# Loads moved between queues, a third place for transposed x, and one more block's products ahead of the table gather

## The reference, cut to what matters

```
# layer 0: base product plus the batch's own adapter, added to x
result = jnp.einsum('bsd,od->bso', x, base_weight) + base_bias
h = jnp.einsum('bsd,brd->bsr', x, lora_A_w[adapter_ids0])
result = result + jnp.einsum('bsr,bor->bso', h, lora_B_w[adapter_ids0])
x = x + result
# layer 1: adapter alone, added to x
Bx = jnp.einsum('bni,bri->bnr', x, L1_cond_B[adapter_ids1])
x = x + jnp.einsum('bnr,bor->bno', Bx, L1_cond_A[adapter_ids1])
```

## Time and profile before

| | us |
|---|---|
| median of 3 runs | 98.51 |
| lowest, highest | 98.11, 99.58 |
| the profiled execution's own time | 97.92 |
| its span, first to last instruction | 95.8 |

### The profile page before, as it was taken

The page is one execution under the profiler, slowest core; times in us unless marked ns, Lnnn a source line. Parts: engine busy times, 40 slices in busy tenths (PEclk is TensorE's granted clock), DMA queues, the critical chain, the costliest instruction groups (busy, mean ns, idle before and its releaser), DMA issues.

```text
span 95.8 us, 2305 instructions
## 1 busy us (share of the span) xinstructions
PE 91.5 (96%) x662; PEld 90.0 (94%) x662; DVE 64.8 (68%) x120; ACT 58.7 (61%) x189; POOL 58.0 (61%) x126
## 2 busy tenths in 40 slices
PE   5999999999999999999999999999999999999980
PEld 5899999999899998999999999999999999999970
DVE  4499799227076468959587877768595868786460
ACT  0074598874588796748494948567584949480210
POOL 6504008850568999999576584959585766808500
PEclk9999999999999999999999999999999999999998
DMA  2999998968896289989996499992836354520205
GB/s 40 312 347 387 374 403 262 281 156 214 215 224 223 53 250 238 310 249 235 203 290 218 70 319 209 238 269 91 228 44 229 34 213 54 200 110 0 110 0 219
DMA packets 16335, 19.45 MB, mean 203 GB/s; under 512 B 1444, under 2 KB 11556, under 8 KB 16164
## 3 DMA queue, kind: packets, MB, share of 16 engines
q1 hardware_dynamic: 15040, 14.04, 50.1%
q0 software_dynamic: 1280, 5.28, 22.1%
q10 hardware_dynamic: 4, 0.00, 0.0%
HBM read 13.47 MB, written 5.84 MB: 202 GB/s over the span
## 4 chain that ended last, share of the span: by engine, by line
PE 90%; DVE 4%; ACT 2%; issue 1%; DVEq 0%; ACTq 0%
PE psum L394 55%; PE psum L440 11%; PE psum L432 4%; PE psum L362 4%; PE psum L480 4%; PE psum L378 4%; PE psum L370 3%; DVE table_rounded L640 3%; PE psum L466 2%; PE psum L414 1%; PE psum L405 1%; PE psum L448 1%; DVE y L679 1%; ACT row_ends L558 1%; ACT table_rounded L558 1%
## 5 line engine op out<-in xcount | busy, mean ns | idle before, releaser
L394 PE MATMUL psum<-wd,xt 128*128 128x256 f32 (+1 forms) x384 | 62.3, 310 | 0.0
L394 PEld LDWEIGHTS psum<-wd,xt 128*128 128x128 f32 x384 | 56.1, 188 | 0.0
L558 ACT ACTIVATE wd<-table_rounded 128x128 fp32r x128 | 27.7, 297 | 14.7 <-PE psum L394 12.5
L339 POOL TENSOR_TENSOR up_rows<-gathered_rows,up_rows 128x512 fp32r<-128x512 f32 x16 | 20.6, 1289 | 14.0 <-ACT up_rows L558 14.0
L322 POOL DMA_INDIRECT gathered_rows<-by_rank,rows x16 | 15.9, 996 | 6.3 <-DMA by_rank<-row_ends 3.8
L640 DVE TENSOR_TENSOR xt<-psum,xt 128x512 fp32r<-128x512 f32 x16 | 11.1, 691 | 6.6 <-ACT xt L558 5.9
L647 DVE STREAM_TRANSPOSE psum<-x_squares 128x512 f32<-128x512 f32 x13 | 14.4, 1110 | 0.0
L440 PE MATMUL psum<-up_rows,u_sel 128*128 128x256 f32 x96 | 14.2, 284 | 0.0
L440 PEld LDWEIGHTS psum<-up_rows,u_sel 128*128 128x128 f32 x96 | 12.8, 190 | 0.2
L659 DVE STREAM_TRANSPOSE psum<-psum 128x128 f32<-128x128 f32 x16 | 5.3, 330 | 11.2 <-PE psum L394 7.8
L332 POOL TENSOR_TENSOR g_sel<-gathered_rows,batch_mask 128x16 f32<-128x16 f32 x64 | 12.1, 227 | 0.9 <-DMA gathered_rows<-by_rank,rows 0.7
(11 more groups left out here) (60 smaller groups left out, 72.1 us busy)
## 6 DMA issues: line engine op xcount, KB each, us to landing
out<-y SPq DMA_DIRECT2D x15, 256.0 KB
x_squares<-in_x SPq DMA_DIRECT2D x8, 256.0 KB
w_rows<-in_L_cond_base_weight SPq DMA_DIRECT2D x4, 256.0 KB, 4.0
bw_rows<-in_L_cond_lora_B_w SPq DMA_DIRECT2D x1, 1024.0 KB, 7.0
a_rows<-in_L_cond_lora_A_w SPq DMA_DIRECT2D x1, 1024.0 KB, 9.2
by_rank<-bw_by_rank SPq DMA_DIRECT2D x4, 256.0 KB
x_squares<-in_x SPq DMA_DIRECT2D x8, 128.0 KB
x_rows<-in_x SPq DMA_DIRECT2D x3, 256.0 KB, 9.3
```

Source lines behind the costliest of these rows:

```text
L339: nc.gpsimd.tensor_tensor(out=up_rows[:, k % 2, LO, :], in0=gathered_rows[:, k % GATHERS, 0:D], in1=up_rows[:, k % 2, HI, :], op=ALU.subtr ...
L394: last = nc.tensor.matmul(bank_of(k, half)[:, start:end], xt[:, k % 2, c, x_part, :], wd[:, w_part, c, col:col + end - start], start=(c == ...
L558: return nc.scalar.activation(dst, src, ACT.Copy)
```

## The change

- SP no longer issues the loads of the broadcast adapter numbers (`ids_all`, two DMAs) and of the bias (`bias_all`). ACT issues them: the numbers before its first drain, the bias after `w_high(0)`. ACT's own reading of the first adapter numbers (`first`) comes after the bias.
- ACT makes a one-column copy (`table_call`) first of all, and drains `b1` in DVE's place.
- On SP, `load_x(1)`, `load_x(2)` and layer 1's A (`l1_a`) are issued ahead of layer 0's A.
- `xt` has three places. x's transpose for block 2 moves ahead of `g`, and block 2's plain half ahead of block 0's adapter half. That half is now made in one piece, with the adapter columns in all four chunks.
- Five `WARM_UPS` in place of six; the two `FILLERS` are gone.
- DVE drains `bw3` after `xt_low(1)`. ACT's `xt_high(2)` comes ahead of the first selections; `select(2, L1)` comes after `up_high(0)`, and `xt_high(3)` after `u_high(0)`. DVE's `xt_low(2)` comes before the reduction, `x_turn(3)` after `own_u(0)`.
- Blocks 4 and 5 of x are loaded apart, and the later groups are issued at other blocks.
- `up(0)` sits after three of block 2's four chunks, where it sat after two.

The core of the diff:

```diff
-WARM_UPS = 6
-FILLERS = 2
+X_SLOTS = 3
+WARM_UPS = 5
-X_GROUPS = ((0, 1), (1, 2), (2, 3), (3, 4), (4, 6), (6, 8), (8, 12), (12, 16))
+X_GROUPS = ((0, 1), (1, 2), (2, 3), (3, 4), (4, 5), (5, 6), (6, 8), (8, 12), (12, 16))
...
-        xt = sb("xt", [P, 2, C, 2, P], F32R)
+        xt = sb("xt", [P, X_SLOTS, C, 2, P], F32R)
...
             sp.dma_start(bw_rows[:, :, :], lora_b.rearrange("n (c p) r -> (n c) p r", p=P)).then_inc(bw_in, 16)
-            sp.dma_start(a_rows[:, :, :], lora_a.rearrange("(g n) r d -> (n r) g d", g=C)).then_inc(a_in, 16)
             load_x(1)
+            load_x(2)
             sp.wait_ge(a1_zeroed, 1)
...
-            load_x(2)
-            for layer, ids_of in ((L0, ids0), (L1, ids1)):
...
+            sp.dma_start(a_rows[:, :, :], lora_a.rearrange("(g n) r d -> (n r) g d", g=C)).then_inc(a_in, 16)
...
             load_x(3)
+            load_x(4)
             for k in range(NBLK - 1):
-                if k in (0, 1, 3, 6):
-                    load_x(4 + (0, 1, 3, 6).index(k))
+                if k in (1, 2, 3, 6):
+                    load_x(5 + (1, 2, 3, 6).index(k))
...
             w_fill(0)
-            keep_warm(FILLERS)
             wait_drained(pe, "b1")
...
             base(0, range(C), halves=[0])
+            x_fill(2)
...
             base(1, range(C), halves=[1])
-            x_fill(2)
+            wait_x(2)
+            wait_drained(pe, "a0")
+            base(2, range(C), halves=[0])
             wait_drained(pe, "c1")
-            base(0, [0, 1], halves=[1], with_d=False, group_check=False)
             wait_d(0)
-            down(0, [0, 1])
-            base(0, [2, 3], halves=[1], group_check=False)
+            base(0, range(C), halves=[1])
             wait_drained(pe, "a3")
             wait_d(1)
             base(1, range(C), halves=[0])
-            wait_x(2)
-            base(2, range(C), halves=[0])
             add_gh(0)
             wait_d(2)
-            base(2, [0, 1], halves=[1])
+            base(2, range(0, C - 1), halves=[1])
             up(0)
-            base(2, [2, 3], halves=[1])
+            base(2, [C - 1], halves=[1])
...
+            act.wait_ge(warm_ready, 1)
+            copy(table_call[:, :], warm[:, 0:1])
+            for layer, ids_of in ((L0, ids0), (L1, ids1)):
+                act.dma_start(ids_all[:, layer, :, :].rearrange("p k b -> p (k b)"),
...
+            wait_filled(act, "b1")
+            copy(b1_cols[:, :, :], chunked(fill_of("b1"))).then_inc(act_drained, 1)
+            w_high(0)
+            act.dma_start(bias_all[:, :], bias.rearrange("(a n) -> a n", a=1).to_broadcast([P, D])).then_inc(bias_in, 16)
...
             select(0, L0, first[0, L0])
             select(1, L0, first[1, L0])
-            xt_high(2)
             select(2, L0)
+            up_high(0)
             select(2, L1)
-            up_high(0)
+            u_high(0)
             xt_high(3)
-            u_high(0)
```

More of the change, by code:

```diff
@@ L381, in c1_part, with base @@
                     last.then_inc(filled, 1)
-            def base(k, chunks, with_d=True, halves=range(2), group_check=True):
+            def base(k, chunks, halves=range(2)):
                 left = W_LEFT[k % 2]
                 regions = [(left, left + HALF, P), (left, left + HALF, P + HALF)]
[L386 to L389, removed]
+                at_half, at = U_AT[k % 2]
+                start = min(at, left)
+                regions[at_half] = (start, start + HALF + P, min(D_AT[k % 2], P + at_half * HALF))
                 for c in chunks:
@@ L393, in base @@
                             start, end, col = regions[half]
-                            last = nc.tensor.matmul(bank_of(k, half)[:, start:end], xt[:, k % 2, c, x_part, :],
+                            last = nc.tensor.matmul(bank_of(k, half)[:, start:end], xt[:, k % X_SLOTS, c, x_part, :],
                                                     wd[:, w_part, c, col:col + end - start],
-                                                    start=(c == 0 and n == 0), stop=(c == C - 1 and n == 2),
-                                                    skip_group_check=not group_check)
-                if with_d and C - 1 in chunks and U_AT[k % 2][0] in halves:
+                                                    start=(c == 0 and n == 0), stop=(c == C - 1 and n == 2))
+                if C - 1 in chunks and U_AT[k % 2][0] in halves:
                     last.then_inc(u_filled, 1)
[L401 to L407, removed]
             def x_fill(k):
@@ L561, in xt_high, with select @@
                 act.wait_ge(xt_filled, k + 1)
+                if k >= X_SLOTS:
+                    act.wait_ge(u_filled, k - X_SLOTS + 1)
+                copy(xt[:, k % X_SLOTS, :, HI, :], chunked(XT)).then_inc(xt_hi_ready, 1)
+            def select(k, layer, n=None):
+                ready, table = ((sel0_ready, table0_rounded), (sel1_ready, table1_rounded))[layer]
+                n = n or adapters_of(act, k, layer)
                 if k >= 2:
                     act.wait_ge(u_filled, k - 1)
[L564 to L570, removed]
                 for b in range(NB):
@@ L717, in _, with lay_bw @@
             xt_low(0)
-            for q in range(4):
+            def lay_bw(q):
                 wait_filled(dve, f"bw{q}")
@@ L721, in _ @@
                                       fill_of(f"bw{q}").rearrange("p (r n c) -> p c n r", n=N0, c=C)).then_inc(dve_drained, 1)
+            for q in range(3):
+                lay_bw(q)
+            xt_low(1)
+            lay_bw(3)
             dve.wait_ge(act_drained, ACT_DRAINS.index("c1") + 1)
             low(table1_rounded[:, :, LO, :, :], c1_by_adapter(), table1_rounded[:, :, HI, :, :]).then_inc(dve_drained, 1)
-            xt_low(1)
             dve.wait_ge(ids_all_in, 32)
@@ L728, in _ @@
                                     op0=ALU.mult).then_inc(ids_f_ready, 1)
+            xt_low(2)
             dve.wait_ge(bias_b1_step, 1)
@@ L740, in _ @@
             turn_u(0)
-            xt_low(2)
+            own_u(0)
             x_turn(3)
-            own_u(0)
+            u_low(0)
             xt_low(3)
-            u_low(0)
             turn_u(1)
```

16 lines of the change are left out of this document (7 added, 9 removed).

## The result

| | before | after |
|---|---|---|
| runs, median (lowest to highest) | 98.68 us (98.11 to 99.58), 4 runs | 102.12 us (101.8 to 103.05), 4 runs |
| profiled execution, its span | 97.92, 95.8 | 101.94, 99.8 |
| mean granted TensorE clock of the span | 0.997 | 0.983 |

The ratio is 1.0355 with a 95% interval of 1.0249 to 1.0461: **slower**, where I had forecast 98.2 us and no change.

What follows compares the result with a forecast made beforehand. Bound: landing of the first gather, plus 7.1 us of POOL, plus PE to the end, unless PE comes later. Gather -0.2 and PE's start -0.1 give 97.6 us; the same step from the 98.51 median gives 98.2, range 96.9 to 99.3.

Steps and rivals of the forecast that it cites:

- Numbers and bias through ACT's queue: Before `g`: moving these loads from SP's queue to ACT's costs 0, bound +0.6 us.
- SP's issue time is not on the path: Before `g`: taking the number and bias loads off SP's queue brings nothing back there.
- Fillers, x's transpose and `g`'s start: Up to `g`: fillers gain 0.45 us, x's transpose for block 2 costs 0.47; `g` starts at 16.06, bounds 15.6 and 16.6.
- From `g`'s drain to usable rows: Drain, store, receipt and gather: 9.15 us stay, less 0.2 from fewer loads of x, bounds 0 and 0.7.
- TensorE waiting 1 us for the gathered rows: Before the first `add_gh`: PE is there at about 28.6, POOL ready at 29.6, so PE's gain becomes a 1 us wait.
- `select(2, L1)` behind the gather: After `add_gh(0)`: this selection is ready at 30.2, `add_gh(0)` done at 29.85, so PE loses another 0.35 us.
- The clock comes later: Rival at the start: fewer warm-ups and no fillers delay full clock, `g` 1.8 us later, 100.0 us; chance 0.08.
- The other two rivals: Gather comes earlier, 97.3 us, chance 0.22; ACT's selections or `bw` come late, 99.0 us, chance 0.11.

Runs made afterwards that it cites:

- e6: The changed kernel with the loads of the adapter numbers and of the bias all back on SyncE's queue; 98.22 us, ratio 0.9976 to before.
- e1: The changed kernel with the two adapter-number loads back on SyncE's queue, last among its loads, the bias still on ScalarE's; 99.27 us, ratio 0.9967.
- e3: The kernel before with one edit: the two adapter-number loads issued early from ScalarE's queue; 100.42 us, ratio 1.0212.
- e7: The changed kernel with the two adapter-number loads on SyncE's queue, right behind the weight's first block; 101.77 us, ratio 1.0339.
- e10: e6 with the loads of x's blocks 3 and 4 held until the table is stored; 100.06 us, ratio 1.0146.
- e4: e1 plus two unused early loads on ScalarE's queue, same shape as the numbers' but from 128 different rows of x; 98.68 us, ratio 1.0019.
- e9: e6 with `g` ahead of x's transpose for block 2; 98.32 us, ratio 0.9951.
- e11: e6 with both the edit of e9 and that of e10; 98.59 us, ratio 0.9976.
- e5: The changed kernel with eight more unread products where TensorE waited for the second weight block; 100.52 us, ratio 1.02.
- e8: e4 with all 128 packets of each unused load reading one row of x; 99.67 us, ratio 1.0134.
- e2: The changed kernel with the two adapter-number loads later on ScalarE's queue, just before the bias, near 6 us; 100.34 us, ratio 1.0193.

## Why the prediction was wrong

**The step that failed** is "Numbers and bias through ACT's queue", which I took at 0 with a bound of +0.6. It cost 102.12 - 98.22 = 3.9 us (after against e6), of which the numbers' loads put `g` 20.17 - 16.33 = 3.8 us late (after against e1). I had priced the bias by its bytes against layer 0's B, and the numbers not at all. I had asked when the transfers are wanted, and not what they would do to those in flight: moved from 6.56 us on SP to 1.7 us on ACT, they fell into the weight's transfer, for which VectorE waits at 4.5 us already. That row is of the weight's first block, which was not late. The second block had little to spare: added at 6.08 before, it was transposed from 7.46, and in after it came at 8.05, 2 us later. "SP's issue time is not on the path" held only as long as the issues were short: e3's chain goes through one of 1.69 us. The Trainium skill (DMA: Bandwidth & Descriptors, Issuing engines are not separate DMA queues) says that DMAs from all issuers share 16 engines and interleave. e7 agrees: the harm is the same from either queue, 8.38 against 8.05. I used that rule to take the step at 0. Transfers that interleave can just as well hold each other up, whoever issues them.

**The other steps**, read in e6, where the failed one is taken out:
- Fillers, x's transpose and `g`'s start: forecast 16.06, measured 16.29, within 15.6 to 16.6. The second set of weight transposes starts at 7.03 in place of 7.46, so the gain of 0.45 came, with one warm-up less. x's transpose ahead of `g` cost 16.29 - 15.61 = 0.68 where I had 0.47.
- From `g`'s drain to usable rows: 9.15 less 0.2. After has 32.87 - 24.02 = 8.85 (24.02 is ACT's drain of the row ends in its chain), e6 28.79 - 20.14 = 8.65, e1 29.24 - 20.18 = 9.06. The forecast of 8.95 lies among them, but they differ by more than the step. The reason, fewer loads of x, was not shown: e10 took them all away and the store was no faster.
- TensorE waiting 1 us for the gathered rows: this failed. It waited 0.35 in after, 0.55 in e1, and in e6 next to nothing (its matmuls end at 25.09 + 4.46 = 29.55, `add_gh(0)` starts at 29.69). It got there later than I took, at 29.55 and not 28.6. The 48 matmuls in front ran in 7.76 us (24 of 256 columns in 3.09, 24 of 384 in 4.46, and 0.21 of waiting for ACT); I had 0.174 us for one of 384 columns, and it took 0.186. It changed the time little, since GpSimd is ready at 28.79 + 0.76 = 29.55 too.
- `select(2, L1)` behind the gather, +0.35: from the first to the third `add_gh` before had 36.19 - 30.09 = 6.10 us, e6 36.12 - 29.69 = 6.43. Right, and `add_gh(2)` at 36.12 lies in the 35.8 to 36.2 that was forecast.

**The rivals.** *The clock comes later* gave 100.0 us from a late rise with fewer warm-ups. Its price, 1.8 us, is near what the clock took (1.6), but by luck, for its cause is another: fewer warm-ups alone left the clock up in 44 of 50 runs (e1, e4, e6, e9, e11). In after it fell in every run, behind the waits that the late weight made, and e5, which fills the first of them, kept it. The six falls among the 50, against none in 51 runs of before, say that the rival can come true now and then; no trace shows where in those runs. The Trainium skill (TensorE: Matmul & The Clock Gate, Part 1) has half rate as the default that activity lifts; after's stretch of half clock behind two waits agrees. It also has a moment that shifts from run to run, and e7's runs of both kinds agree. The other two rivals did not come about.

**What stays open.** Why the early same-place reads hold back the DMA engines, while before's two loads, issued at 6.56 among others, harmed nothing visible (DMA share 1.03 from 10 to 14 us; 255 packets under 512 bytes went by between 14 and 15 us, where after had 62 to 66 a us from 4 to 7). Which pattern of waits brings the half clock: e8 waited 1.73 us and kept it, after waited 1.29 and 0.69 and lost it in every run. What sets the time from the store of the row ends to the gather, 3.8 to 4.6 us in most kernels and 5.3 in e2; with it, why e9's earlier `g` did not move the gather. And whether the new order of loads delays later blocks of x, as in e1's profile.

## What to carry to other kernels

Ask of a load that is moved earlier which transfers it will fall among, and whether somebody waits for them already or soon; its bytes did not price it here. A small broadcast read, many packets from one place in DRAM, is better issued behind the loads that the start waits for (e1, e6), or timed there first. Work that covers a wait (warm-ups, fillers) should be weighed by what it would be worth if the transfer came 2 us late.

## What the runs showed that I had not expected

- Two loads of 32 KB whose packets all read the same 256 bytes, issued at 1.7 us, cut the traffic from 4 to 6 us from 280 or more to between 45 and 135 GB/s (e1 against after, e3, e5, e7, e8). They took 6.1 us to land in after and 4.3 in e7. The same shape from 128 rows took 4.2 and left 281.
- The DMA engines read as idle in that stretch (share 0.27 to 0.44) while the weight landed 2 us late, so the low share was no sign of spare capacity here.
- TensorE's waits of 1.3 to 1.7 us, at the start or before the first `add_gh`, were followed by a stretch at half clock in some kernels and runs and not in others; such runs mostly read a mean of 0.978 to 0.983 over the span, and in after it cost 1.6 us.
